# Rotary partners by a shuffle of partitions instead of by second products, in a four-layer transformer kernel

## The reference, cut to what matters

```python
def _rope(x, cos, sin):                      # layer 1's attention, R = 8
    x1 = x[..., :R // 2]
    x2 = x[..., R // 2:R]
    rot = jnp.concatenate([x1 * cos - x2 * sin, x2 * cos + x1 * sin], axis=-1)
    ...
q = _rope(q, cos, sin)
k = _rope(k, cos, sin)
scores = jnp.einsum('nthd,nshd->nhts', q, k) * scale + bias
```

```python
xr = xh.reshape(xh.shape[:-1] + (d // 2, 2))
x0, x1 = (xr[..., 0], xr[..., 1])
rot = jnp.stack([x0 * cos - x1 * sin, x0 * sin + x1 * cos], axis=-1)
...
q = jnp.concatenate([q_nope, _rope(q_rope)], axis=-1)
k = jnp.concatenate([kv, _rope(k_rope)], axis=-1)
att = jnp.einsum('bhqd,bhkd->bhqk', q, k) / jnp.sqrt(jnp.float32(D))
```

## Time and profile before

| | us |
|---|---|
| median of 3 runs | 2881.08 |
| lowest and highest | 2880.33, 2889.78 |
| the profiled execution | 2875.41 |
| its span, first to last instruction | 2874.1 |
| TensorE busy | 2496.8 (87%) |
| VectorE busy | 1688.0 (59%) |
| ScalarE busy | 1384.6 (48%) |
| GpSimd busy | 786.5 (27%) |
| mean granted TensorE clock | 0.95 |

### The profile page before, as it was taken

How to read it: one execution, slowest core, us unless ns; L and a number is a source line. 1 busy time by engine, 2 the same in 40 slices (tenths; PEclk the granted TensorE clock), 3 DMA queues, 4 the chain that set the end, 5 groups by cost and what they waited for, 6 DMA issues and landing times. The chain is left out here.

```text
span 2874.1 us, 63682 instructions
## 1 busy us (share of the span) xinstructions
PE 2496.8 (87%) x27230; PEld 1666.6 (58%) x27373; DVE 1688.0 (59%) x4552; ACT 1384.6 (48%) x2370; POOL 786.5 (27%) x684
## 2 busy tenths in 40 slices
PE   4889898878878898888998898888888888899999
PEld 2466565655555555455576677665555555566666
DVE  4766666666554557777765556555566464555332
ACT  3475335665444226776743344433444556554332
POOL 2321446453121222111012232222110121354353
PEclk9899999999898989999999999999999899899999
DMA  3001333000000001000000000000010000021142
GB/s 107 18 1 32 76 85 82 17 17 10 3 2 2 4 12 42 18 12 1 10 1 30 17 17 17 17 22 22 15 63 7 7 1 1 22 73 48 52 125 67
DMA packets 50459, 84.72 MB, mean 29 GB/s; under 512 B 9536, under 2 KB 24768, under 8 KB 49792
## 3 DMA queue, kind: packets, MB, share of 16 engines
q1 hardware_dynamic: 50176, 80.64, 10.3%
HBM read 77.99 MB, written 2.62 MB: 28 GB/s over the span
## 5 line engine op out<-in xcount | busy, mean ns | idle before, releaser
L456 PE MATMUL psum<-halves_held 128*128 128x512 bf16 x561 | 153.3, 387 | 10.8 <-issue 7.7
L899 DVE TENSOR_TENSOR c_L3f_h<-c_L3f_h,psum 128x512 f32<-128x512 f32 (+1 forms) x112 | 75.9, 685 | 136.4 <-PE psum L880 115.4
L864 POOL TENSOR_TENSOR c_L3f_h<-c_L3f_h,c_L3f_spread 128x512 f32<-128x512 f32 x96 | 121.6, 1301 | 102.2 <-DVE c_L3f_h L899 53.4
L889 ACT ACTIVATE c_L3f_h<-psum 128x512 f32<-128x512 f32 (+1 forms) x112 | 65.0, 594 | 130.4 <-PE psum L876 130.1
L909 PEld LDWEIGHTS psum<-weights,c_L3f_h 128*128 128x128 f32 (+1 forms) x896 | 110.1, 196 | 22.3 <-issue 18.8
L880 PE MATMUL psum<-c_L3f_xT,weights 128*128 128x512 f32 (+1 forms) x224 | 115.4, 600 | 0.5 <-ACT c_L3f_h L889 0.5
L876 PE MATMUL psum<-c_L3f_xT,weights 128*128 128x512 f32 (+1 forms) x224 | 114.5, 597 | 0.0
L909 PE MATMUL psum<-weights,c_L3f_h 128*128 128x128 f32 (+1 forms) x896 | 113.5, 282 | 0.0
L864 POOL TENSOR_TENSOR c_L0f_h<-c_L0f_h,c_L0f_spread 128x512 f32<-128x512 f32 x64 | 80.6, 1292 | 86.8 <-DMA c_L0f_spread<-scratch 82.4
L456 PEld LDWEIGHTS psum<-halves_held 128*128 128x128 bf16 x701 | 66.3, 100 | 64.5 <-issue 18.8
L2049 DVE TENSOR_REDUCE c_L2x_mx<-psum 128x8 f32<-128x1024 f32 x64 | 77.6, 1221 | 41.9 <-PE psum L1944 41.2
(11 more groups left out here) (635 smaller groups left out, 6822.1 us busy)
## 6 DMA issues: line engine op xcount, KB each, us to landing
c_L0f_spread<-scratch SPq DMA_DIRECT2D x64, 256.0 KB, 5.6
c_L3f_spread<-scratch SPq DMA_DIRECT2D x32, 512.0 KB, 5.6
c_L2f_spread<-scratch SPq DMA_DIRECT2D x64, 128.0 KB, 3.1
c_L3f_spread<-scratch SPq DMA_DIRECT2D x64, 128.0 KB, 6.0
c_L0x_ctxT<-ctxT SPq DMA_DIRECT2D x8, 384.0 KB, 8.2
c_L1x_ctx<-ctx SPq DMA_DIRECT2D x16, 192.0 KB, 2.4
c_L2x_ctxT<-ctxT SPq DMA_DIRECT2D x8, 384.0 KB, 4.4
c_L3x_ctxT<-ctxT SPq DMA_DIRECT2D x8, 384.0 KB, 3.8
```

Source lines behind the costliest of these rows:

```text
L456: nc.tensor.matmul(j.psum[:, bank, :], j.half["ident"], j.half["take"], start=True, stop=True)
L864: nc.gpsimd.tensor_tensor(h, h, j.m["spread"][:, f, :], ALU.mult).then_inc(*j.up("mixed"))
L889: nc.scalar.activation(j.m["h"][0:rows, f, :], j.psum[0:rows, 1 + 2 * f % 3, 0:j.tok], ACT.Silu).then_inc(*j.up("silu"))
L899: nc.vector.tensor_tensor(h, h, j.psum[0:rows, 1 + (2 * f + 1) % 3, 0:j.tok], ALU.mult).then_inc(*j.up("gated"))
```

## The change

The second products and their weights go. VectorE makes the partners itself. It multiplies the one product by the cosines and, again from the same bank, by the sines, whose signs are now laid out for the partner, and then exchanges partitions of the second result within each group of 32 by a stream shuffle, in place. GpSimd's adds wait for the shuffles. In L2f the key's second result has a buffer of its own (`ktwin`). L1a's values go to bank 1, so they no longer wait for the turned keys; L2f's second pair of queries goes to bank 3 and waits for `va` only. The shuffles are steps of their own: in L1a after both turns, in L2f the keys' after the first pair's turn and the queries' after the second pair's. ORDER is searched anew over the whole program; PLAN is the same. In all the program has 96 fewer fp32 matmuls (16 of 128x512, 80 of 128x256), 64 shuffles (48 of 128x512, 16 of 128x256) and 127 more idle matmuls (892 against 765 of this shape, the masks of L2261 among both).

```diff
-perm8 = rope_partner(16, 8)
-        ("wq", P, P, ...), ("wqp", P, P, lambda a: a["L1_attn_w_qkv"][:D][perm8].T),
+        ("wq", P, P, ...),
+PARTNER8 = [f - f % 8 + (f + 4) % 8 for f in range(32)]
+PARTNER2 = [f ^ 1 for f in range(32)]
...
-    c["sin8"] = np.sin(ang) * np.where(p % 8 < 4, -1.0, 1.0)[:, None]
+    c["sin8"] = np.sin(ang) * np.where(p % 8 < 4, 1.0, -1.0)[:, None]
...
 def pe_L1a(nc, j):
-    for n, w in enumerate(("wk", "wkp")):
-        put = t.matmul(psum[:, n, :], j.weight(w), m["xT"][:], start=True, stop=True)
-    put.then_inc(*j.up("keys"))
+    t.matmul(psum[:, 0, :], j.weight("wk"), m["xT"][:], start=True, stop=True).then_inc(*j.up("keys"))
     yield
...
-    t.wait_ge(*j.at("k_turns", 1))
     for n in range(j.tiles):
-        put = t.matmul(psum[:, 0, n * P:(n + 1) * P], ...
+        put = t.matmul(psum[:, 1, n * P:(n + 1) * P], ...
...
 def pool_L1a(nc, j):
-    g.wait_ge(*j.at("k_turns", 1))
+    g.wait_ge(*j.at("k_twins", 1))
...
 def dve_L1a(nc, j):
-    v.tensor_tensor(by_seq(m["twin"][:]), by_seq(psum[:, 1, :]), sin, ALU.mult).then_inc(*j.up("k_turns"))
+    v.tensor_tensor(by_seq(m["twin"][:]), by_seq(psum[:, 0, :]), sin, ALU.mult).then_inc(*j.up("k_turns"))
...
+    yield
+    v.wait_ge(*j.at("k_turns", 1))
+    v.stream_shuffle(m["twin"][:], m["twin"][:], PARTNER8).then_inc(*j.up("k_twins"))
+    yield
+    v.wait_ge(*j.at("q_turns", 1))
+    v.stream_shuffle(m["twin2"][:], m["twin2"][:], PARTNER8).then_inc(*j.up("q_twins"))
     yield
     v.wait_ge(*j.at("values", 1))
...
 def pe_L2f(nc, j):
-    t.matmul(psum[:, 0, tok:2 * tok], j.weight("wkp"), m["xT"][:], start=True, stop=True).then_inc(*j.up("keys"))
...
-    for pair, (turn, twin) in enumerate(((1, 3), (0, 2))):
-        for bank, w, (seen, count) in ((turn, "wqr", ("k_turns", 1) if pair else ("kx", 1)), (twin, "wqp", ("qx", 1) if pair else ("va", 1))):
-            yield
-            t.wait_ge(*j.at(seen, count))
...
+    for pair in range(2):
+        yield
+        t.wait_ge(*(j.at("va", 1) if pair else j.at("kx", 1)))
+        for n in range(2):
+            cols = slice((2 * pair + n) * P, (2 * pair + n + 1) * P)
+            put = t.matmul(psum[:, 1 + 2 * pair, n * tok:(n + 1) * tok], j.weight("wqr")[:, cols], m["xT"][:], start=True, stop=True)
         put.then_inc(*j.up("queries"))
     yield
+    t.wait_ge(*j.at("qx", 1))
     t.wait_ge(*j.at("q_turns", 2))
...
 def pool_L2f(nc, j):
-        g.wait_ge(*j.at("q_turns", pair + 1))
+        g.wait_ge(*j.at("q_twins", pair + 1))
...
 def dve_L2f(nc, j):
-        v.tensor_tensor(by_seq(m["twin"][:, pair, :]), by_seq(psum[:, twin, :]), sin, ALU.mult).then_inc(*j.up("q_turns"))
+        v.tensor_tensor(by_seq(m["twin"][:, pair, :]), by_seq(psum[:, 1 + 2 * pair, :]), sin, ALU.mult).then_inc(*j.up("q_turns"))
+        if pair == 0:
+            yield
+            v.wait_ge(*j.at("k_turns", 1))
+            v.stream_shuffle(m["ktwin"][:], m["ktwin"][:], PARTNER2).then_inc(*j.up("k_twins"))
+    for pair in range(2):
+        yield
+        v.wait_ge(*j.at("q_turns", pair + 1))
+        v.stream_shuffle(m["twin"][:, pair, :], m["twin"][:, pair, :], PARTNER2).then_inc(*j.up("q_twins"))
...
 ORDER = (
-    "VdddDDDLlDdKkqqQQvddDdDDLldDPkAGPApaPApaPpaKgGPPVppVAgpvvaVvVVDVvDvdDddLPDvQqAGlpdagpaKPpagkApppvvaPAPPvvGPVVAvdvddlVVpa"
+    "QVDDDdLdDdldKkqqdvddlDDdDkppLDaaKgPpaPgpAGppAvvavPAGPPvvPVvdVddlpagpAaVVdVpakgppQqQPDVDDLDPAApvvKGavvvPAPPGPVVAdddlVppag"
```

More of the change, by code:

```diff
@@ L198, in constant_table @@
     c["cos32"] = np.cos(ang)
-    c["sin32"] = np.sin(ang) * np.where(p % 2 == 0, -1.0, 1.0)[:, None]
+    c["sin32"] = np.sin(ang) * np.where(p % 2 == 0, 1.0, -1.0)[:, None]
     same = p[:, None] // S == p[None, :] // S
@@ L232 @@
           "out_b": "logits", "outT_b": "combT", "o_turned_b": "route", "denom_b": "x_normed", "att_b": "gained",
-          "products": "part", "composed": "o_turned"}
+          "products": "part", "composed": "o_turned", "k_twins": "split", "q_twins": "cleared"}
 class Context:
@@ L1746, in pe_L1a @@
     t.wait_ge(*j.at("features", 1))
-    for n, w in enumerate(("wk", "wkp")):
-        put = t.matmul(psum[:, n, :], j.weight(w), m["xT"][:], start=True, stop=True)
-    put.then_inc(*j.up("keys"))
+    t.matmul(psum[:, 0, :], j.weight("wk"), m["xT"][:], start=True, stop=True).then_inc(*j.up("keys"))
     yield
-    for n, w in enumerate(("wq", "wqp")):
-        put = t.matmul(psum[:, 2 + n, :], j.weight(w), m["xT"][:], start=True, stop=True)
-    put.then_inc(*j.up("queries"))
+    t.matmul(psum[:, 2, :], j.weight("wq"), m["xT"][:], start=True, stop=True).then_inc(*j.up("queries"))
     yield
-    t.wait_ge(*j.at("k_turns", 1))
     for n in range(j.tiles):
-        put = t.matmul(psum[:, 0, n * P:(n + 1) * P], m["xT"][:, n * P:(n + 1) * P], j.weight("wv"), start=True, stop=True)
+        put = t.matmul(psum[:, 1, n * P:(n + 1) * P], m["xT"][:, n * P:(n + 1) * P], j.weight("wv"), start=True, stop=True)
     put.then_inc(*j.up("values"))
@@ L2235, in pe_L2f @@
     put.then_inc(*j.up("latent"))
-    t.matmul(psum[:, 0, 0:tok], j.weight("wkr"), m["xT"][:], start=True, stop=True)
-    t.matmul(psum[:, 0, tok:2 * tok], j.weight("wkp"), m["xT"][:], start=True, stop=True).then_inc(*j.up("keys"))
+    t.matmul(psum[:, 0, 0:tok], j.weight("wkr"), m["xT"][:], start=True, stop=True).then_inc(*j.up("keys"))
     yield
@@ L2248, in pe_L2f @@
     put.then_inc(*j.up("queries"))
-    for pair, (turn, twin) in enumerate(((1, 3), (0, 2))):
-        for bank, w, (seen, count) in ((turn, "wqr", ("k_turns", 1) if pair else ("kx", 1)), (twin, "wqp", ("qx", 1) if pair else ("va", 1))):
-            yield
-            t.wait_ge(*j.at(seen, count))
-            for n in range(2):
-                cols = slice((2 * pair + n) * P, (2 * pair + n + 1) * P)
-                put = t.matmul(psum[:, bank, n * tok:(n + 1) * tok], j.weight(w)[:, cols], m["xT"][:], start=True, stop=True)
+    for pair in range(2):
[4 more added lines that the diff above has]
+            put = t.matmul(psum[:, 1 + 2 * pair, n * tok:(n + 1) * tok], j.weight("wqr")[:, cols], m["xT"][:], start=True, stop=True)
         put.then_inc(*j.up("queries"))
     yield
+    t.wait_ge(*j.at("qx", 1))
     t.wait_ge(*j.at("q_turns", 2))
```

170 lines of the change are left out of this document (81 added, 89 removed).

## The result

The changed kernel takes 2869.81 us as the median of nine runs (2859.7 to 2886.0), against 2881.08 us for nine runs of the kernel before. The ratio is 0.9949 [0.9925, 0.9974]: 0.51% faster, some 11 to 15 us, where 20.4 us were forecast. The profiled execution took 2870.87 us.

What follows compares the result with a forecast made beforehand. TensorE's work was taken to bound L2f mostly, with waits inside jobs for the rest. Products -37.4, delays +16 and +6, VectorE's queue +3, clock -8 summed to -20.4 us: 2881.1 to 2860 us, range 2830 to 2894.

Steps and rivals of the forecast that it cites:

- own range: Whole kernel: the forecast's narrower range, 2843 to 2871 us, from the delay and clock terms.
- The clock term: Mainly L1a, L2x, L3x: 127 added idle matmuls win back clock, -8 us, bounds -47 and +27.
- the clock falls: Rival, L2f: less TensorE work lowers the clock from 0.96 to 0.88; +10 us, 2891 us; chance 0.05.
- The delays: Shuffles delay L2f's query adds (+16 us), L1a's copies (+6 us) and VectorE's queue elsewhere (+3 us).
- half the jobs pay: L2f: eight of sixteen jobs lose 2.0 us as query adds end later, +16 us; bounds 10 and 32.
- The products: L1a and L2f: dropping the second products takes 48.3 us of TensorE work, -37.4 us on the path.
- The share of 77%: L2f: 42.8 of 55 us of query products stand on the chain; share borrowed for key products and L1a.
- The rows that were to tell: Profile after: signs expected if right, on TensorE's busy time, L2f's stretch, shuffle time, query-add waits and clock.
- four signs against the forecast: Shuffle over 1.2 us; L2f exponential waits above 40 us; query add on most jobs' chain; gain in blocks without shuffles.
- The fourth: Blocks without shuffles: a gain lying there would make it the order's and not the change's.
- VectorE as the bound: Rival, L2f and L1a: TensorE waits for VectorE's shuffles; +39 us if all paid, midway 2901 us; chance 0.12.
- Saving turns into waiting: Rival: all sixteen L2f jobs pay 2.0 us, no clock gain; +3.6 us, 2885 us; chance 0.15.

Runs made afterwards that it cites:

- e1: The changed kernel's code under the order of the kernel before, each shuffle directly behind its own turn: 2884.8 us, ratio 1.0003 to the kernel before.
- e5: The change under the old order, with idle matmuls of the same length in place of the removed products: 2892.0 us, ratio 1.0035 to the kernel before.
- e10: The changed kernel plus three idle matmuls before each L2f transpose group and six in each L1a job: 2858.0 us, ratio 0.9900 to the kernel before.
- e2: The kernel before, with its second products and no shuffles, under the new order: 2896.4 us, ratio 1.0064 to the kernel before.
- e8: The changed kernel without the 64 shuffles and the waits for them: 2852.7 us, ratio 0.9902 to the kernel before.
- e7: The changed kernel under its new order, but each shuffle directly behind its own turn: 2880.1 us, ratio 0.9997 to the kernel before.
- e9: The changed kernel run again with nothing altered: 2868.5 us, ratio 0.9944 to the kernel before.
- e3: The kernel before with the new order for the first 209 steps (the first block) only: 2877.0 us, ratio 0.9976 to the kernel before.
- e11: The kernel before plus three idle matmuls ahead of each group of L2f's transposes: 2888.6 us, ratio 1.0022 to the kernel before.
- e6: The changed kernel plus three idle matmuls ahead of each of L2f's 32 groups of transposes: 2858.4 us, ratio 0.9916 to the kernel before.

## Why the prediction was right, and where it was off

The direction, the range and the own range held: the forecast was 2860 us, the time is 2869.8. The range (2830 to 2894 us) was wide enough for most of the rivals, and the own range ends at 2871. The size was off: 20.4 us forecast, 11 to 15 measured. The runs show two terms of the sum as mis-sized, in opposite directions. And part of the hit is luck. The sum had the gain where the products went, L1a and L2f, and nothing for the order in other blocks; in the profiles those stretches together are 2 to 9 us shorter than before, and the first block some 15.

**The clock term had the wrong sign.** I forecast -8 us, since idle matmuls were added in stretches of low clock. Measured, the clock of the runs fell from 0.947 to 0.942, which at 20.7 us per 0.01 is about +10 us. What I saw as added to L1a came to less than what was taken away there (31 idle matmuls, 6.7 us, for 13.9 us of products): its clock went from 0.88 to 0.85 and L2f's from 0.96 to 0.92. L2x rose from 0.95 to 0.97 and L3x hardly, 0.87 to 0.88. The rival "the clock falls" had the mechanism right for the old order and got 0.05; its clock price was 30 us for L2f alone and too high, and its +10 us still had my -8 us in it; without them it is +18. The runs showed its mechanism three times: e1 (clock down, gain gone), e5 (clock back with idle work), e10 (idle work in the waits, clock up, time lower). Under the new order it isn't shown: e2 has the products and in L2f the clock of 0.92 too. By the Trainium skill (TensorE: Matmul & The Clock Gate, Part 1) the array is throttled by default and activity releases it; e1 and e5 agree.

**The delays cost less.** I had +16 us for GpSimd's adds, +6 us in L1a and +3 us for the queue, 25 us in all. e8 measured 13.5 us for all of it. The term that failed is "half the jobs pay": TensorE waited 6.5 us for the query add, in four places, where half of 16 jobs would be 16 us, and e7, which starts the first add earlier, is no faster at equal clock. The job shown above has a reason: 5 us of other work stand between add and scores.

**The products.** -37.4 us for 48.3 us of work. Under the new order, e2 against the changed kernel, the exchange with its shuffles is worth 33 us, so the products, with the waits for banks that went with them, some 33 + 13 = 46 us. The share of 77% was read under the old order; under the new one nearly all of the 48.3 us came back, but the freed waits are in that number. But the same order costs 0.64% with the products in. Together, at equal clock, the change is worth 2886 - 2863 = 23 us; with the clock's +10 that is the 13 measured. A sum of -37.4 + 13.5 and +10 gives -14 as well; that it fits is no proof of the 37.4, since exchange and order can't be priced apart (16 us under the old order at equal clock, 36 under the new).

**The rows that were to tell.** TensorE's busy time fell less than 48 us: right, 11. L2f's stretch 10 us or more shorter: not shown. From its first copy into `xT` to its last it took 583.3 us, 6 us less than before (589.4), but 590.0 in the changed kernel's second profile (e9). The shuffle 0.6 to 0.8 us: right, 0.73, and 0.44 for 128x256 (0.77 and 0.50 forecast). As time taken from VectorE all shuffles come to 33.5 us by e8, and not 45, since VectorE's next operation starts 0.62 us after a 128x512 one's start. The Trainium skill's price (VectorE: DVE Perf Modes, "The perf-mode tier table") had given an estimate of 0.60 us for 512 elements and 34 us in all. The 0.62 and the 33.5 us agree with it; the 0.73 us, which is what the adds wait for, doesn't, and there the trace decides. Waits for the query add 2 to 10 us: right in kind, 6.5. The clock rises in L1a and L3x: wrong in L1a. Of the four signs against the forecast three stayed away (no shuffle over 1.2 us, 25.4 us of waits for the exponential, four jobs with the add on the chain). The fourth appeared, a gain in a block without shuffles, 14.4 us in the first and in nearly all profiles with its new order. Of the whole kernel's time e3 finds some 7 us of it, between none and all. The sign was to make the gain the order's and not the change's. It is the order's as to its place, but e2 shows that the order without the change loses 0.64%.

**The rivals.** VectorE as the bound is refuted: e8 gives all shuffles 13.5 us, where it needed 77. "Saving turns into waiting" is what e1's time looks like, and a reader of that profile alone would find it: waits for the exponential of 28.5 us. But e5 and the equal-clock times put e1's lost gain on the clock and not on those waits.

**What stays open.** Which part of the new order fits the shuffles, and why it costs 12 us at equal clock with the products in. Why L3x takes longer under it. How far the new order, and how far the missing products, lowered the clock. The carrying to an equal clock takes a slope found within kernels as valid between them; that e11 loses by the matmuls with which e6 is at least no slower says that what they cost differs by kernel, and the estimate can't separate the two.

## What to carry to other kernels

Where TensorE's clock is below full in a stretch with waits, price the removal of TensorE work twice: by the time it frees and by the clock that the rest may lose. Here 48 us of work off, 13 us of time gained with the order searched anew, and nothing without. Look at the waits that are left, and try a few short idle matmuls inside them, counted by experiment: three in L2f with six in L1a paid 0.4%, six in L2f cost 0.6% over three, and in the kernel with the higher clock three cost 0.2%. Don't place a gain of 0.5% by the milestones of two single profiles: read the same milestone in every profile that has the stretch, and test an order and the code that it was searched for as one.
